# Two layers of transformer on one core: loads, projection and plain attention in one program, weights quantised and slots cleared there

## What is computed

```python
x = x + attention_0(layernorm(x))   # 16 heads of 8, softmax(q k^T / sqrt(8)) v, no output projection
x = x + ffn_0(layernorm(x))         # silu(gate) * up, then down; inputs and weights rounded to FP4 in blocks of 16
x = x + attention_1(layernorm(x))   # q and k turned by position for the numerator only, causal, w_out, b_out
x = x + ffn_1(layernorm(x))         # 8 experts, each token sent to its best 2, 512 slots an expert and choice
```

## Time and profile before

| | |
|---|---|
| median of 3 runs | 1942.66 us (1941.76 to 1943.98) |
| the profiled execution | 1942.2 us, span from first to last instruction 1940.2 us |
| TensorE (PE) busy | 1641.1 us, 85% |
| ScalarE (ACT) busy | 1455.8 us, 75% |
| VectorE (DVE) busy | 1182.5 us, 61% |
| GpSimd (POOL) busy | 245.2 us, 13% |
| mean granted TensorE clock | 0.949 of 2.4 GHz |

### The profile page before, as it was taken

One profiled execution on the slowest core, in us unless ns is written; L12 is line 12 of the kernel. 1 busy time (PEld: TensorE's weight loads), 2 busy tenths in 40 slices (PEclk: granted clock), 3 DMA queues, 4 the chain that ended last, 5 costly groups with the idle time before them and its releaser, 6 DMA issues. The chain is left out here.

```text
span 1940.2 us, 33298 instructions
## 1 busy us (share of the span) xinstructions
PE 1641.1 (85%) x12863; PEld 631.9 (33%) x12948; DVE 1182.5 (61%) x2119; ACT 1455.8 (75%) x2516; POOL 245.2 (13%) x259
## 2 busy tenths in 40 slices
PE   5489999999999999943788898888889888883995
PEld 3122222222222222232234333433333333222674
DVE  8899999999999998368264544455354533213220
ACT  4167787777787778722999999999999999992221
POOL 4400000000000000012000100010001113321466
PEclk9589999999999999966999999999999999996998
DMA  4300011100000000052211221113012223231433
GB/s 138 122 2 26 30 35 34 32 26 27 26 26 27 26 26 5 2 205 92 71 50 49 67 97 50 50 42 119 19 36 80 94 66 110 96 117 33 144 61 31
DMA packets 68430, 115.84 MB, mean 60 GB/s; under 512 B 9305, under 2 KB 54213, under 8 KB 62640
## 3 DMA queue, kind: packets, MB, share of 16 engines
q1 hardware_dynamic: 58416, 92.87, 15.0%
q0 software_dynamic: 9856, 20.83, 3.8%
HBM read 71.49 MB, written 42.14 MB: 59 GB/s over the span
## 5 line engine op out<-in xcount | busy, mean ns | idle before, releaser
L752 ACT ACTIVATE probs<-psS 128x512 f32<-128x512 f32 x1024 | 556.4, 596 | 187.7 <-PE psS L656 186.3
L771 DVE TENSOR_REDUCE max_of_halves<-psM 128x2 f32<-128x1024 f32 x512 | 617.7, 1222 | 46.3 <-PE psM L625 16.8
L1504 ACT ACTIVATE exps<-cpsS 128x1024 bf16<-128x1024 f32 x512 | 540.7, 1090 | 26.6 <-PE cpsS L1274 26.2
L1274 PE MATMUL cpsS<-rotary_stack 128*128 128x512 bf16 x952 | 288.1, 386 | 80.1 <-ACT exps L1504 31.0
L676 PE MATMUL psO<-probs,plain_v 128*9 128x256 f32 x4096 | 317.0, 381 | 4.9 <-issue 2.3
L1514 ACT ACTIVATE cprobs<-cpsS 128x1024 f32<-128x1024 f32 x256 | 277.6, 1085 | 20.0 <-PE cpsO L1307 17.3
L1254 PE MATMUL cpsS<-rotary_stack 128*128 128x512 bf16 (+3 forms) x755 | 192.8, 331 | 63.2 <-ACT exps L1504 37.5
L625 PE MATMUL psM<-plain_top 64*128 64x512 bf16 x1024 | 212.3, 395 | 32.0 <-DVE max_of_halves L771 22.7
L656 PE MATMUL psS<-plain_top 64*128 64x512 bf16 x1024 | 213.3, 388 | 7.4 <-issue 6.1
L656 PE MATMUL psS<-plain_rest 64*128 64x512 bf16 x1024 | 207.6, 378 | 0.0
L1307 PE MATMUL cpsO<-cprobs,rotary_v 128*9 128x512 f32 (+3 forms) x1536 | 154.6, 490 | 0.6 <-DVE rotary_sums L1820 0.6
(11 more groups left out here) (283 smaller groups left out, 1663.7 us busy)
## 6 DMA issues: line engine op xcount, KB each, us to landing
rotary_stack<-q_parts SPq DMA_DIRECT2D x48, 192.0 KB
rotary_stack<-k_parts SPq DMA_DIRECT2D x48, 192.0 KB
rotary_stack<-q_rot_parts SPq DMA_DIRECT2D x48, 192.0 KB
rotary_stack<-k_rot_parts SPq DMA_DIRECT2D x48, 192.0 KB
tokens_taken<-sent_rows POOLq DMA_DIRECT2D x8, 1036.0 KB, 17.1
plain_top<-q_parts SPq DMA_DIRECT2D x64, 96.0 KB
plain_top<-k_parts SPq DMA_DIRECT2D x64, 96.0 KB
e_x<-tokens_taken SPq DMA_DIRECT2D x8, 518.0 KB, 9.6
```

Of the source, the lines that this page charges most:

```text
L752: act.activation(pr[n % SLOTS_P][:, h, :], psS[u % RING][:, :], ACT.Exp, scale=SCALE).then_inc(s_e, 1)
L771: dve.tensor_reduce(mh[g % 2][:, :, hh, t, kh:kh + 1].rearrange("p e o -> p (e o)"), psM[n % 2][:, :, :], AX.X, ALU.max).then_inc(s_r, 1)
L1274: ins = pe.matmul(to[:, kh, :], q[:, x, y_ * P:(y_ + 1) * P], k[:, x, kh * CH:(kh + 1) * CH], start=True, stop=True)
L1504: act.activation(ex[d % EX][:, :, :], psS[n % 3][:, :, :], ACT.Exp, scale=SCALE, accum_out=den[:, at:at + 1]).then_inc(s_e, 1)
```

## The change

The load phase and the projection become a class `Projection`, whose parts run at the head of plain attention's program, engine by engine. Two barriers, SP's wait for the last stores ahead of plain attention and the loads' end ahead of the projection go. The buffers share space: normalised and turned rows lie in what later holds probabilities, rests and parts in what later holds the sums, and the PSUM banks are those of the scores and the sum. There are two banks for units in place of three, and four store slots in place of five.

Batch 0 leads: its statistics, deviations (without the square root on ScalarE; three Newton steps on VectorE, `inverse_deviation`) and normalising come first, then the statistics of the others, then units 0 to 3, then the deviations of the other 24 tiles and chunks 2 and 3. From chunk 2 on the tiles of chunk c + 2 are normalised behind the rests of chunk c. SP loads three copies a unit from unit 4 on, ahead of the unit's store.

The FFN's weights are no longer quantised in the projection, but behind `merge(14)` in the last group (`quantise`). `first_rows` moves ahead of `merge(14)`, right behind the shift parts of the last group. GpSimd clears the slots in plain attention, behind the clearing of the rotary operands: 32 writes of 128 x 2 rows in place of 8 of 128 x 8.

```diff
-FILLS = 8
+FILLS = 32
...
-    def quantise_some(self, dve, u):
-        if u < 2:
-            return
...
+    def quantise(self, dve):
+        ch = Chain(dve, self.s_wd)
+        dve.wait_ge(self.s_w, 80)
+        for part in range(2):
+            v, amax, rs, magic = self.operands(part)
             if part:
                 dve.wait_ge(self.s_wq, 1)
-            ch.link(dve.tensor_reduce(amax, v, AX.X, ALU.max, apply_absolute_value=True))
-            ch.link(dve.tensor_scalar(amax, amax, 1.0 / 6.0, 1e-12, ALU.mult, ALU.max))
-        elif i == 1:
-            ch.link(dve.reciprocal(rs, amax))
-            ch.link(dve.tensor_scalar(rs, rs, NUDGE, None, ALU.mult))
-        elif i == 2:
-            ch.link(dve.tensor_tensor(v, v, bc(rs, QB), ALU.mult))
-            ch.link(dve.tensor_scalar(magic.bitcast(I32), v.bitcast(I32), EXP_BITS, None, ALU.bitwise_and))
-        elif i == 3:
-            ch.link(dve.tensor_scalar(magic, magic, 1.0, HALF_MAGIC, ALU.max, ALU.mult))
-            ch.link(dve.tensor_tensor(v, v, magic, ALU.add))
-        else:
-            ch.link(dve.tensor_tensor(v, v, magic, ALU.subtract))
+            ch.link(round_fp4(dve, ch, v, amax, rs, magic))
             dve.tensor_tensor(v, v, bc(amax, QB), ALU.mult).then_inc(self.s_wq, 1)
...
-def load_phase(p, x, fw, w_gate, w_up, w_down):
-    nc = p.nc
...
-    RING = 3
-    STORES = 5
...
+class Projection:
+    RING, STORES = 3, 4
...
+        self.psT, self.psQ = banks[0:2], banks[2:4]
...
+        def turn(ci):
+            to = bank(use["x", ci])
+            for i in range(TC):
+                pe.wait_ge(self.s_n, ci * TC + i + 1)
+                ins = pe.transpose(to[:, i * P:(i + 1) * P], self.xn[:, ci * TC + i, :], p.ident[:, :])
+            ins.then_inc(self.s_t, 1)
...
+        def products(ci):
+            pe.wait_ge(self.s_tk, use["x", ci] + 1)
+            rhs = self.xt[:, ci * CH:(ci + 1) * CH]
+            for k in range(2):
+                u = ci * 2 + k
+                if u >= 2:
+                    pe.wait_ge(self.s_rest, u - 1)
+                pe.matmul(self.psQ[u % 2][:, :], self.w[:, k, :], rhs, start=True, stop=True).then_inc(self.s_q, 1)
...
+        turn(0)
+        turn(1)
+        pe.wait_ge(self.s_wk, 3)
+        products(0)
+        products(1)
+        turn(2)
+        turn(3)
+        for ci in range(2, NCH):
+            products(ci)
+            if ci + 2 < NCH:
+                turn(ci + 2)
...
+        def first_part(u):
+            if u >= self.STORES:
+                act.wait_ge(self.s_st[u % self.STORES], 16 * (u // self.STORES))
+            act.wait_ge(self.s_q, u + 1)
+            act.activation(self.part[u % self.STORES][:, 0, :], self.psQ[u % 2][:, :], ACT.Copy).then_inc(self.s_p0, 1)
+        def second_part(u):
+            act.wait_ge(self.s_rest, u + 1)
+            act.activation(self.part[u % self.STORES][:, 1, :], self.rest[:, u % self.RING, :], ACT.Copy).then_inc(self.s_p1, 1)
+        keep_inputs(0)
+        keep_inputs(1)
         for ci in range(NCH):
+            first_part(2 * ci)
+            if ci not in (0, 2):
+                second_part(2 * ci - 1)
+            first_part(2 * ci + 1)
+            second_part(2 * ci)
+            keep_values(ci)
+            if ci == 1:
+                second_part(3)
+                keep_inputs(2)
+                keep_inputs(3)
+            elif 2 <= ci < NCH - 2:
+                keep_inputs(ci + 2)
+        second_part(self.U - 1)
...
+        stats(0)
+        deviations(range(TB))
+        normalise(range(TB))
+        for b in range(1, B):
+            stats(b)
+        for u in range(4):
+            take_rest(u)
+        deviations(range(TB, T))
+        normalise(range(TB, 2 * TB))
+        for ci in range(2, NCH):
+            take_rest(2 * ci)
+            take_rest(2 * ci + 1)
+            if ci + 2 < NCH:
+                normalise(range((ci + 2) * TC, (ci + 3) * TC))
...
+        stacks.clear(pool)
+        for u in range(self.U):
+            pool.wait_ge(self.s_p1, u + 1)
+            pool.tensor_tensor(self.part[u % self.STORES][:, 2, :], self.rest[:, u % self.RING, :],
+                               self.part[u % self.STORES][:, 1, :], ALU.subtract).then_inc(self.s_p2, 1)
...
+        for b in range(B):
+            sp.dma_start(p.X[:, b * TB:(b + 1) * TB, :], xv[:, b * TB:(b + 1) * TB, :]).then_inc(self.s_x[b], 16)
+            if b == 0:
+                sp.dma_start(self.raw[:, :, :], w_qkv.rearrange("(t p) d -> p t d", p=P)).then_inc(self.s_w, 16)
+        self.fw.load(sp, w_gate, w_up, w_down)
...
+        SHARE = 3
+        for u in range(self.U):
+            ci, k = u // 2, u % 2
+            b, at = ci * CH // N, ci * CH % N
+            if u == 4:
+                for i in range(4):
+                    sp.wait_ge(self.s_st[i], 16)
+                sp.wait_ge(stacks.s_clear, stacks.CLEARS)
+            if u >= 4:
+                for to, src, s_ld in first_group[:SHARE]:
+                    sp.dma_start(to, src).then_inc(s_ld, 16)
+                del first_group[:SHARE]
+            sp.wait_ge(self.s_p2, u + 1)
+            sp.dma_start((p.qs, p.ks)[k][:, b * D:(b + 1) * D, at:at + CH].rearrange("j p n -> p j n"),
+                         self.part[u % self.STORES][:, :, :]).then_inc(self.s_st[u % self.STORES], 16)
+        self.wait_stored(sp)
...
-            pe.wait_ge(s_oz, 1)
+            project.tensor(pe)
...
+                            if g == 0:
+                                act.wait_ge(project.s_p1, project.U)
+                                act.wait_ge(project.s_p2, project.U)
+                                project.wait_stored(act)
...
+            project.vector(dve)
+            dve.wait_ge(project.s_rest, project.U)
...
+                    if g == G - 1:
+                        dve.wait_ge(s_mg, 2 * (G - 2))
+                        first_steps = first_rows()
                 else:
                     merge(g)
                     if g == G - 2:
-                        dve.wait_ge(s_mg, 2 * (g + 1))
-                        first_rows()
+                        dve.wait_ge(s_fr, first_steps)
+                        fw.quantise(dve)
...
+            project.gpsimd(pool)
             rotary.clear(pool)
+            project.wait_stored(pool)
+            pool.memset(zeros[:, :, :], 0.0).then_inc(s_zm, 1)
+            pool.wait_ge(s_zm, 1)
+            pool.memset(zeros[:, :, WHO:WHO + 1], 1.0e9).then_inc(s_zm, 1)
+            pool.wait_ge(s_zm, 2)
+            rows = p.taken.rearrange("(a p b) d -> a p b d", a=FILLS, p=P)
+            for i in range(FILLS):
+                pool.dma_start(rows[i, :, :, :], zeros[:, :, :]).then_inc(s_zs, 16)
...
-                if kind == "r" and n == 0:
-                    dve.wait_ge(s_zs, 16 * FILLS)
...
-            zeros = send[:, 0:2, :, :].rearrange("p b t d -> p (b t d)")
-            pool.memset(zeros, 0.0).then_inc(s_zm, 1)
...
-            for i in range(FILLS):
-                pool.dma_start(rows[i, :, :], zeros).then_inc(s_zs, 16)
...
-            load_phase(p, z, fw, w_gate, w_up, w_down)
...
-                project_phase(p, w_qkv0, plain, fw, xn)
-                softmax_phase(p, plain, stacks, fw, xn)
+                s_zm, s_zs = ctx.enter_context(nc.semaphore("zeros_made")), ctx.enter_context(nc.semaphore("zeros_stored"))
+                softmax_phase(p, plain, stacks, fw, xn, z, w_qkv0, w_gate, w_up, w_down, s_zm, s_zs)
```

More of the change, by code:

```diff
@@ L199, in take_stats @@
         dve.bn_stats(p.stats[:, t, :], p.X[:, t, :])
-def norm_steps(p, dve, ch, mv, rstd, out, s_std):
-    for t in range(T):
-        n = ch.inc(dve.bn_aggr(mv[:, t, :], p.stats[:, t, :]))
-    dve.wait_ge(ch.sem, n)
-    ch.inc(dve.tensor_scalar(rstd[:, :], mv[:, :, 1], EPS, None, ALU.add))
-    dve.wait_ge(s_std, 1)
-    ch.link(dve.reciprocal(rstd[:, :], rstd[:, :]))
-    for t in range(T):
-        ch.inc(dve.tensor_scalar(out[:, t, :], p.X[:, t, :], mv[:, t, 0:1], rstd[:, t:t + 1],
-                                 ALU.subtract, ALU.mult))
@@ L550, in inverse_deviation, with softmax_phase @@
         ch.link(dve.scalar_tensor_tensor(rstd[:, :], tmp[:, :], 1.5, rstd[:, :], ALU.add, ALU.mult))
-def softmax_phase(p, stacks, rotary, fw, xn):
+def softmax_phase(p, stacks, rotary, fw, xn, x, w_qkv, w_gate, w_up, w_down, s_zm, s_zs):
     nc = p.nc
@@ L608, in softmax_phase @@
         s_fr = sem("first_rows")
+        project = Projection(p, c, sb, sem, stacks, fw, xn, arena, area,
+                             [psS[0][:, :], psS[1][:, :], psS[2][:, :], psO[:, :]])
+        project.s_made = sem("constants_made")
         block = c.enter_context(nc.Block())
@@ L844, in _ @@
                 stacks.fill(pool, g % 2, g)
+            pool.wait_ge(s_zs, 16 * FILLS)
         @block.sync
         def _(sp):
+            project.sync(sp, x, w_qkv, w_gate, w_up, w_down)
             stacks.load_tops(sp, 1)
```

327 lines of the change are left out of this document (124 added, 203 removed).

## The result

| | before | changed |
|---|---|---|
| median of 18 runs each | 1941.57 us (1940.71 to 1945.61) | 1945.68 us (1944.18 to 1947.63) |
| ratio, 95% interval | | 1.0019 (1.0012 to 1.0026) |
| span of the profiled execution | 1940.2 us | 1944.9 us |

The changed kernel is slower by 0.19%, about 4 us. Read the profile in the order in which the prediction went.

The account below looks back on a forecast made before the run. VectorE's first maximum was taken to set the front, ScalarE's exponentials the pace up to 820 us. 1942.2 - 1.5 (front) - 2.8 (late program) = 1937.9, plus 0.5 for the median: 1938.4 us, range 1931 to 1944.

Parts of the forecast that it names:

- The writes in their new place: GpSimd's 32 zero writes in plain attention: issued by 98 us, before the shift at 103.5; cost 0, at most 3.0 us.
- the third rival: Zero writes still in flight at 103 us delay the first scores by up to 3.0 us; 1941.4 us, chance 0.08.
- Late program: 2.8 us saved: Late start: without the zero writes the output bias lands sooner, TensorE's turn of w_qkv moves from 832.93 to 830.1.
- The second rival: Late start: the output bias load is slow by itself, so only 1.5 us are saved; 1941.2 us, chance 0.25.
- Front saves 1.5 us: Load phase and projection: VectorE's first maximum at 62.5 us against 64.05, after the longer projection takes back 5.5.
- The handover: Projection to attention without barrier or store wait: first maximum 0.7 us after the last rest; 7.0 us saved there.
- the stretched small step: Batch 0's deviations on VectorE: first small step waits out most of a GpSimd memset, 1.3 us added.
- F of unit 6: Projection: ScalarE's first part (F) of unit 6, forecast to start at 38.2 us.
- the wait of unit 15 for a store: Projection's end: unit 15 needs unit 11's store slot, with four slots for five; its first part starts at 60.4 us.
- four N beside the third: Projection loop: VectorE normalises four tiles (N) after waiting out GpSimd's last parts of units (thirds); 1.05 us.
- The fourth rival: TensorE stays at 1.2 GHz through the projection, 8.6 us more, first maximum at 71; 1947.0 us, chance 0.08.
- Last group: 0: Last group of plain attention: rounding first rows and weights hides in VectorE's idle time, 17 us to spare; cost 0.

Follow-up runs that it names:

- bias_apart_before: Kernel before, with loads of both biases and the router on their own semaphore, so TensorE's turn waits only for w_qkv and w_out; ratio to before 0.9984.
- clock_kept: Changed kernel with zero writes moved behind group 2's values, plus useless TensorE products in the 21 to 27 us pause and behind four chunks; ratio to before 0.9986.
- changed_again: The changed kernel itself, unedited, run once more on another chip; ratio to the kernel before 1.0021.
- writes_large: Changed kernel with the same zeros at the same place as 8 writes of 1036 KB in place of 32 of 259 KB; ratio to before 0.9998.
- normalise_ahead: Changed kernel with zero writes moved behind group 2's values and chunk c+2 normalised ahead of chunk c's rests; ratio to before 0.9951.
- six_slots: Changed kernel with writes behind group 2, normalising ahead of rests, biases on their own semaphore, six store slots for four; 1926.48 us against 1943.01, ratio 0.9911.

## Why the prediction was wrong

Forecast 1938.4, in a range from 1931 to 1944; it became 1945.68, on the other side of the kernel before. Point by point:

- **"The writes in their new place": the step that failed.** I took 0, "since the issue alone is done 5 us earlier". Issue is not landing. The 32 issues ended at 98.3, as forecast, the bytes at 112.1, 8 us after the shift was sent. The mechanism stood there as the third rival, with its condition (a write of 259 KB takes over 0.7 us: at 290 GB/s it takes 0.9), but with a chance of 0.08 and a price that was too small. "Up to 3.0 us" came from what the late load had lost in the earlier trace rows, and that load had lost nothing to the writes. Measured: 5.1 us in one trace, 5.3 in the other. A sum of bytes would have given the danger: 8.5 MB from 81 us on, at the 369 GB/s that the earlier trace rows shows for the stores, end at 104.0 at the best, behind the 103.5 that I had for the shift's issue; with the 0.9 MB of loads that the same stretch carries it is 106.4. What the sum does not give is how long a small load is held by the bytes in front of it: 3.0 us without a packet and 2.0 us of taking turns.
- **"Late program: 2.8 us saved": failed.** The second rival (the load is slow by itself) was true. bias_apart_before shows it in the kernel before, writes and all. What I had put against the step, that the writes moved almost nothing in the earlier trace rows, was the better argument.
- **"Front saves 1.5 us": nearly right in the first trace, too much on the mean.** First maximum 62.5 forecast, 63.17 in the first trace, 63.4 over seven. The kernel before stands at 63.7 over three. That leaves 0.4 us saved. The handover came out: 0.6 us from the end of the last rest to the first maximum in place of 7.7 (0.7 forecast). But the longer projection takes back 6.2 of those 7.1 us in the first trace, where I had 5.5. Many steps came out: the stretched small step (1.35 for 1.3), chunks 2 and 3 normalised at 28.7 (29.5), F of unit 6 at 38.19 (38.2), F of unit 12 at 56.32 (55.3), the wait of unit 15 for a store (1.18 us), four N beside the third at 1.96 in place of 1.05. F of unit 6 is right by luck in part: its chunk was ready 0.8 us early, and its product took about 0.9 us longer than I had it. What I had wrong is the clock. I let units 4 and 5 alone run at 1.2 GHz; in these traces between one and a half and four of the six chunks behind the pause do. The fourth rival (0.08) had this at its worst, 8.6 us on top of the forecast; the seven traces stand from 0.8 us better to 2.8 us worse than the forecast, 0.9 worse on the mean. With the clock held, in clock_kept, the first maximum came at 59.34; the forecast without its 2.4 us for a lower clock gives 60.1. So the loop's other steps were about right, and the clock cost 4.0 us on the mean in place of 2.4.
- **"Last group: 0": right.** The rounding ended 18.4 us ahead of the next merge, and took 11.3 us where I had 12.

The balance of the mean: -0.4 (front) + 5.1 (shift) + 0 (late) = +4.7 us; the medians say +4.1, the ratio's interval +2.3 to +5.0.

## What to carry to other kernels

A transfer is not hidden when its issue is: add up the bytes in flight and see where they end against the next small load on the path, and put bulk writes where the next load behind them has a whole stage of slack. Where a loop passes through four engines, look for the step that needs nothing of this round and do it in the wait for the round's first result; that gave about seven microseconds here, while the merged program, whose removed barrier saved 7.1 at the handover, gave most of it back in a slower loop and kept less than one. And one semaphore for several loads makes the first reader wait for the slowest of them, needed or not.

## What the runs showed of the hardware that was not expected

- A load of three times 8 KB, issued by SyncE while GpSimd's writes were in flight, lost 5.1 us in two ways. For 3.0 us longer than without the writes (4.3 us after its issue in place of 1.2) none of its 102 packets moved. From then on it was served between the writes: while these lasted, its packets of 256 bytes each had a write packet of 4144 bytes (0.17 us) close behind, so that the load's own packets took 3.3 us from the first to the last in place of 1.4. changed_again shows the same (first packet after 4.4 us). In writes_large all 102 moved between 106 and 108, with 0.12 MB of the writes beside them. The Trainium skill (DMA: Bandwidth & Descriptors, Queues, rings and completion order) says that an engine takes turns between its queues, packet by packet. From 108.4 us on the trace agrees with that. The Trainium skill lets a packet hold, in the same section, about 9 to 17 descriptors, so it need not be what the profile counts as one, and whether the 3.0 us before were the wait for such a packet, or something else, stays open.
- Writes with rows of 2.1 KB moved 299 to 349 GB/s, with rows of 8.3 KB 408 to 425, at the same busy share of the DMA engines (1.00 to 1.03). The row and the size of a write (259 and 1036 KB) changed together, so which of them does it is not shown.
- The granted clock fell and rose at different chunks in seven executions of the same projection, in which TensorE paused 1.2 to 2.0 us a chunk and 5.8 us once; with most of these pauses filled (0.7 to 1.2 us were left) it held 1.00. In normalise_ahead and six_slots, where up to 40 us only the long pause is left, slow products stood at units 4 and 5 alone (1.94 and 1.91 us; 1.94 and 1.20 us).
- A 64 KB load whose 128 rows all come from one row of the source took 4.3 to 5.3 us in the fourteen traces as the fifth of seven loads, with DMA engines nearly idle (share 0.06 in the earlier trace rows); an equal one two places earlier took 2.3 to 4.5, and less than the fifth in each trace. Why was not tried.
